# Graph attention: scores from turned rows in one product, four pairs a step, all steps written out

## What is computed

```python
def _L1_gnn_ref(x, edge_index, edge_attr, Wq, bq, Wk, bk, Wv, bv, We, Wskip, bskip, gamma, beta):
    ...
    q_all = x @ Wq.T + bq
    k_all = x @ Wk.T + bk
    v_all = x @ Wv.T + bv
    e = edge_attr @ We.T
    q = q_all[dst]
    k = k_all[src] + e
    v = v_all[src] + e
    scale = 1.0 / jnp.sqrt(jnp.asarray(d, dtype=x.dtype))
    alpha = (q * k).sum(-1) * scale
    amax = jax.ops.segment_max(alpha, dst, num_segments=N)
    ex = jnp.exp(alpha - amax[dst])
    denom = jax.ops.segment_sum(ex, dst, num_segments=N)
    w = ex / denom[dst]
    agg = jax.ops.segment_sum(v * w[:, None], dst, num_segments=N)
    out = agg + x @ Wskip.T + bskip
```

## Time and profile before

| | |
|---|---|
| median of 3 runs | 7149.32 us (7145.72 to 7151.49) |
| profiled execution | 7175.0 us, its span 7173.4 us |
| mean granted clock of TensorE | 0.811 of full |
| TensorE busy (PE) | 5774.2 us, 80% |
| VectorE busy | 4790.4 us, 67% |
| ScalarE busy | 3097.9 us, 43% |
| GpSimd busy | 1945.7 us, 27% |
| the chain that ended last | PE 40%, DVE 30%, issue 17%, another queue 6% |

### The profile page before, as it was taken

One profiled execution on the slowest core, in us unless ns is written; L12 is line 12 of the kernel. 1 busy time (PEld: TensorE's weight loads), 2 busy tenths in 40 slices (PEclk: granted clock), 3 DMA queues, 4 the chain that ended last, 5 costly groups with the idle time before them and its releaser, 6 DMA issues.

```text
span 7173.4 us, 145546 instructions
## 1 busy us (share of the span) xinstructions
PE 5774.2 (80%) x45481; PEld 4074.9 (57%) x45482; DVE 4790.4 (67%) x14785; ACT 3097.9 (43%) x8500; POOL 1945.7 (27%) x2110
## 2 busy tenths in 40 slices
PE   1499995577777777777777748999999999988998
PEld 0377773355555555555555526666666666654665
DVE  3888884565666666666666639999999999952001
ACT  0255554344444444444444434555555555520000
POOL 4011100455555555555555510000000000000110
PEclk6699997666666656656666668999999999978999
DMA  5255542222222222222222200000000000005664
GB/s 164 81 181 180 182 162 77 51 62 61 62 60 63 62 61 62 60 63 64 60 63 60 58 28 21 4 4 4 4 4 4 4 4 4 4 2 181 205 204 139
DMA packets 375578, 505.33 MB, mean 70 GB/s; under 512 B 258173, under 2 KB 303357, under 8 KB 355054
## 3 DMA queue, kind: packets, MB, share of 16 engines
q1 hardware_dynamic: 289631, 356.27, 15.3%
q0 software_dynamic: 82592, 141.23, 8.5%
q10 hardware_dynamic: 2738, 0.54, 0.0%
HBM read 341.26 MB, written 169.04 MB: 71 GB/s over the span
## 4 chain that ended last, share of the span: by engine, by line
PE 40%; DVE 30%; issue 17%; another core or an unknown queue 6%; ACT 2%; DVEq 2%; POOL 1%; DMA 1%; SPq 1%; ACTq 0%; POOLq 0%
PE psum L1213 36%; DVE R L708 8%; DVE HT L708 5%; DVE l L708 4%; DVE H L1101 3%; PE psum L1402 2%; DVE junk L1112 2%; DVE ACC L1086 2%; PE psum L1479 1%; DVEq L434 1%; DVE cols_pc L708 1%; DVE att L1075 1%; ACT H L1543 1%; DVE att L1112 1%
## 5 line engine op out<-in xcount | busy, mean ns | idle before, releaser
L1543 ACT ACTIVATE H<-psum 128x256 f32<-128x256 f32 (+2 forms) x1853 | 681.7, 391 | 1654.2 <-remote 565.7
L1213 PE MATMUL psum<-R 128*128 (+3 forms) x10946 | 1161.2, 260 | 85.5 <-DVE R L708 40.6
L1213 PE MATMUL psum<-R,HT 128*128 128x384 bf16 x6076 | 1084.3, 326 | 59.8 <-DVEq L1202 59.8
L1543 ACT ACTIVATE R<-psum 128x512 f32<-128x512 f32 (+4 forms) x1597 | 844.6, 543 | 537.9 <-PE psum L1213 488.1
L1213 PEld LDWEIGHTS psum<-R,G 128*128 128x128 bf16 x11840 | 735.0, 98 | 567.7 <-issue 334.9
L1213 PEld LDWEIGHTS psum<-R 128*128 128x128 bf16 x10946 | 834.9, 111 | 361.1 <-issue 158.0
L1213 PE MATMUL psum<-H 128*128 128x139 f32 (+1 forms) x3328 | 768.3, 352 | 322.2 <-DVE ACC L1086 153.3
L1213 PE MATMUL psum<-R,l 128*128 128x512 f32 (+1 forms) x1924 | 954.2, 578 | 67.0 <-DVE HT L708 64.5
L642 POOL DMA_INDIRECT H<-gather_table,idx_f x832 | 803.7, 966 | 590.4 <-remote 205.8
L642 POOL DMA_INDIRECT G<-gather_table,idx_f x832 | 787.2, 946 | 623.9 <-PE psum L1213 275.4
L1075 DVE TENSOR_TENSOR att<-att,col_f 128x1 f32<-128x1 f32 x1664 | 264.9, 159 | 960.5 <-remote 372.6
(11 more groups left out here) (227 smaller groups left out, 8124.9 us busy)
## 6 DMA issues: line engine op xcount, KB each, us to landing
adjacency_blocks<-HT SPq DMA_DIRECT2D x74, 1568.0 KB, 5.4
HT<-adjacency_blocks SPq DMA_DIRECT2D x50, 1568.0 KB, 6.6
H<-local_dst_pairs SPq DMA_DIRECT2D x104, 512.0 KB
R<-adjacency_blocks SPq DMA_DIRECT2D x24, 1568.0 KB, 6.5
G<-gather_table,idx_f POOLq DMA_INDIRECT x832
H<-gather_table,idx_f POOLq DMA_INDIRECT x832
node_sums<-G POOLq DMA_DIRECT2D x148, 64.0 KB
attr_pairs<-H SPq DMA_DIRECT2D x13, 640.0 KB, 7.0
```

The lines of the kernel that those rows point to most:

```text
L1213: return nc.tensor.matmul(o, lhs_t, rhs, start=start, stop=stop)
L1543: return nc.scalar.activation(o, a, f, **kw)
```

## The change

The attention stage is rewritten, in its arithmetic and in its order.

- **Scores by one product.** TensorE turns each gathered slot (`GT`, 128 rows, and the 11 extra columns as `GX`), ScalarE copies both, and the scores of a pair come straight as rows: queries of the window, turned (128 deep), times `GT`, plus the turned extras (11 deep) times `GX`, both float32, into one PSUM region. The one-hot matrices, `Q3`, VectorE's score product, the split into parts and its turning are gone. The queries' own product is now made turned, 13 blocks of up to four windows, into `QK` and `QX`.
- **Queries by transfer.** No engine reads a window's number but SyncE: it copies each pair's queries (128x128) and extras (11x128) from `QK` and `QX` into one of 16 places, six steps of four pairs ahead.
- **Sums by transfer.** VectorE adds into a ring of eight places (`sums`), each from the one before. SyncE writes every pair's place to `attention_sums` in DRAM, at the window's number for a window's last pair and at one of eight spare places otherwise (`put`). At the end the sums come back into `ACC` in four parts.
- **Corrections.** The differences of old and new maximum are made by VectorE for four pairs at once, and ScalarE takes one exponential for the four.
- **Four pairs a step, written out.** 416 steps and five more for the tail, no hardware loop. In step k TensorE makes the sum products of group k - 4, turns the exponentials of group k - 3, makes the scores of group k - 1 and turns the rows of group k. VectorE interleaves, pair by pair, the maximum of group k - 1 with the addition of group k - 4. The gathers need no copy of their indices.

The core of the diff (indentation cut by eight):

```diff
-Q3 = r1.bitcast(bf16)[:, 0:3 * W * FX].rearrange("p (t w f) -> p t w f", t=3, w=W)
+
 QT = accflat[:, 0:NP]
-member = r2b[:, 0:2 * CH * P].rearrange("p (u j e) -> p u j e", u=2, j=CH)
+QK = QT.rearrange("p (w n) -> p w n", n=P)
+QX = r1[0:X1, 0:NP].rearrange("p (w n) -> p w n", n=P)
+at = NP
+GT = r1[:, at:at + 2 * GR * P].rearrange("p (u j e) -> p u j e", u=2, j=GR)
+at += 2 * GR * P
+GX = r1[0:X1, at:at + 2 * GR * P].rearrange("p (u j e) -> p u j e", u=2, j=GR)
+at += 2 * GR * P
+masked = r1[:, at:at + 3 * GR * P].rearrange("p (j e) -> p j e", e=P)
...
+sums = hflat[:, at:at + AR * FX].rearrange("p (j f) -> p j f", f=FX)
+assert at + AR * FX <= NH
+queries = R2[:, 0:CH * P].rearrange("p (j n) -> p j n", n=P)
+at += AR * FX
+extras = [l2[0:X1, j * P:(j + 1) * P] for j in range(8)]
+extras += [accflat[0:X1, NP + j * P:NP + (j + 1) * P] for j in range(6)]
+extras += [hflat[0:X1, at + j * P:at + (j + 1) * P] for j in range(2)]
...
+    def load_rows(c):
+        if c >= 2:
+            sp.wait_ge(s_mem, c - 1)
+        rows = loc_p[c * CH:(c + 1) * CH, :].rearrange("(a j) e -> a (j e)", a=1)
+        sp.dma_start(locrow[:, c % 2, :], rows.broadcast_to([P, CH * P])).then_inc(s_lr[c % 2], 16)
+    def load_attrs(m):
+        if m >= 4:
+            sp.wait_ge(s_use, 8 * (m - 3))
+        h = m % 2 * CH // 2
+        sp.dma_start(G_att[m // 2 % 2][:, h:h + CH // 2, F + 1:FX],
+                     ea_p[m * CH // 2:(m + 1) * CH // 2, :].rearrange("j (e a) -> e j a", a=ED)).then_inc(s_ea[m % 4], 16)
+    def put_sums(k):
+        places = load_places(GR * k, GR)
+        for j in range(GR):
+            p = GR * k + j
+            sp.wait_ge(s_acc, p + 1)
+            sp.dma_start(sums_d.rearrange("(w n) f -> n w f", n=P)[:, bass.ds(places[j], 1), :].rearrange("n a f -> n (a f)"),
+                         sums[:, p % AR, :]).then_inc(s_fl[p % AR], 16)
+    def load_queries(k):
+        if k >= 4:
+            sp.wait_ge(s_row, k - 3)
+        numbers = load_windows(ENG.SP, GR * k, GR)
+        for j in range(GR):
+            a = (GR * k + j) % CH
+            sp.dma_start(queries[:, a, :], QK[:, bass.ds(numbers[j], 1), :].rearrange("p a n -> p (a n)")).then_inc(s_qw[k % 4], 16)
+            sp.dma_start(extras[a], QX[:, bass.ds(numbers[j], 1), :].rearrange("p a n -> p (a n)")).then_inc(s_qw[k % 4], 16)
+    for c in range(2):
+        load_rows(c)
+    for m in range(4):
+        load_attrs(m)
+    sp.wait_ge(s_qh, NB)
+    sp.wait_ge(s_qx, NB)
+    for k in range(6):
+        load_queries(k)
+    for k in range(GN):
+        put_sums(k)
+        if k + 6 < GN:
+            load_queries(k + 6)
+        if k % 4 == 3 and k // 4 + 2 < PC // CH:
+            load_rows(k // 4 + 2)
+        if k % 2 == 1 and k // 2 + 4 < PC * 2 // CH:
+            load_attrs(k // 2 + 4)
+    for k in range(AR):
+        sp.wait_ge(s_fl[k], 16 * (PC // AR))
+    for c in range(4):
+        w0_, w1_ = 4 * (NB * c // 4), min(W, 4 * (NB * (c + 1) // 4))
+        sp.dma_start(ACC[:, w0_:w1_, :], sums_d[w0_ * P:w1_ * P, :].rearrange("(w n) f -> n w f", n=P)).then_inc(s_back[c], 16)
...
-    for u in range(2):
-        gather(0, u, table, G_att)
-    loop(pool, gather, PC, table, G_att, first=2 * CH)
+    for p in range(PC):
+        if p % GR == 0 and p >= 2 * CH:
+            pool.wait_ge(s_use, p - 2 * CH + GR)
+        edge = bass.IndirectOffsetOnAxis(ap=idx_c[:, p:p + 1], axis=0)
+        pool.indirect_dma_start(out=slot(p)[:, 0:F], out_offset=None, in_=table, in_offset=edge).then_inc(s_g[p // GR % 8], 16)
...
+    for b, (w0_, n) in enumerate(BLK):
+        v.wait_ge(s_q, b + 1)
+        v.tensor_copy(QX[:, w0_:w0_ + n, :], psum[0:X1, 6 + b % 2, 0:n * P].rearrange("p (w n) -> p w n", n=P)).then_inc(s_qx, 1)
...
-    def attention_vector(i, k):
-        p = i + k
...
+    for k in range(GN + 5):
+        for j in range(GR):
+            p, q = GR * (k - 1) + j, GR * (k - 4) + j
+            if k - 1 in range(GN):
+                if p:
+                    v.wait_ge(s_min, p)
+                tt(oldm[:, p % CH:p % CH + 1], newm[:, (p - 1) % CH:(p - 1) % CH + 1], aux_c[:, p:p + 1],
+                   ALU.max).then_inc(s_nmo, 1)
+            if k - 4 in range(GN):
+                if j % 2 == 0:
+                    v.wait_ge(s_use, q + 2)
+                if j == 0:
+                    v.wait_ge(s_c, k - 3)
+                if q:
+                    v.wait_ge(s_acc, q)
+                if q >= AR:
+                    v.wait_ge(s_fl[q % AR], 16 * (q // AR))
+                v.scalar_tensor_tensor(sums[:, q % AR, :], sums[:, (q - 1) % AR, :], corr[:, q % CH:q % CH + 1],
+                                       psum[:, 6 + j // 2, j % 2 * FX:(j % 2 + 1) * FX], ALU.mult, ALU.add).then_inc(s_acc, 1)
+            if k - 1 in range(GN):
+                if j == 0:
+                    v.wait_ge(s_row, k)
+                    if k >= 4:
+                        v.wait_ge(s_et, k - 3)
+                    if p % CH == 0:
+                        v.wait_ge(s_mem, p // CH + 1)
+                v.wait_ge(s_nmo, p + 1)
+                v.tensor_tensor_reduce(out=masked[:, p % (3 * GR), :], in0=psum[:, 3 + (k - 1) % 2, j * P:(j + 1) * P],
+                                       in1=penalty[:, p // CH % 2, p % CH, :], scale=1.0, scalar=oldm[:, p % CH:p % CH + 1],
+                                       op0=ALU.add, op1=ALU.min, accum_out=newm[:, p % CH:p % CH + 1]).then_inc(s_min, 1)
+        if k - 1 in range(GN):
+            p = GR * (k - 1)
+            at = slice(p % CH, p % CH + GR)
+            v.wait_ge(s_min, p + GR)
+            tt(dif[:, at], newm[:, at], oldm[:, at], ALU.subtract).then_inc(s_dif, 1)
+            v.wait_ge(s_dif, 2 * k - 1)
+            v.scalar_tensor_tensor(dif[:, at], aux_c[:, p:p + GR], -1.0, dif[:, at], ALU.mult, ALU.min).then_inc(s_dif, 1)
+        if k % 4 == 3 and k // 4 + 1 < PC // CH:
+            mask_rows(k // 4 + 1)
...
-    def attention_tensor(i, k):
-        p = i + k
...
+    for b, (w0_, n) in enumerate(BLK):
+        if b >= 2:
+            t.wait_ge(s_qx, b - 1)
+            t.wait_ge(s_qh, b - 1)
+        mm(psum[:, 4 + b % 2, 0:n * P], C[:, 0:F], QT[:, w0_ * P:(w0_ + n) * P])
...
+    for k in range(GN + 5):
+        if k - 4 in range(GN):
+            t.wait_ge(s_etc, k - 3)
+            if k >= 5:
+                t.wait_ge(s_acc, GR * (k - 4))
+            for j in range(GR):
+                mm(psum[:, 6 + j // 2, j % 2 * FX:(j % 2 + 1) * FX], ET[:, j, :], slot(GR * (k - 4) + j)).then_inc(s_use, 1)
+        if k - 3 in range(GN):
+            t.wait_ge(s_exp, GR * (k - 2))
+            if k >= 4:
+                t.wait_ge(s_etc, k - 3)
+            for j in range(GR):
+                last_ins = nc.tensor.transpose(bank4(5)[:, j, :], masked[:, (GR * (k - 3) + j) % (3 * GR), :], ident[:, :])
+            last_ins.then_inc(s_et, 1)
+        if k - 1 in range(GN):
+            t.wait_ge(s_gt, k)
+            if k >= 3:
+                t.wait_ge(s_min, GR * (k - 2))
+            t.wait_ge(s_qw[(k - 1) % 4], 128 * ((k - 1) // 4 + 1))
+            for j in range(GR):
+                o, a = bank4(3 + (k - 1) % 2)[:, j, :], (GR * (k - 1) + j) % CH
+                mm(o, queries[:, a, :], GT[:, (k - 1) % 2, j, :], stop=False)
+                last_ins = mm(o, extras[a], GX[:, (k - 1) % 2, j, :], start=False)
+            last_ins.then_inc(s_row, 1)
+        if k in range(GN):
+            t.wait_ge(s_g[k % 8], 64 * (k // 8 + 1))
+            if k % 2 == 0:
+                t.wait_ge(s_ea[k // 2 % 4], 16 * (k // 8 + 1))
+            if k >= 1:
+                t.wait_ge(s_gt, k)
+            for j in range(GR):
+                nc.tensor.transpose(bank4(k % 2)[:, j, :], slot(GR * k + j)[:, 0:F], ident[:, :])
+            for j in range(GR):
+                last_ins = nc.tensor.transpose(bank4(2)[0:X1, j, :], slot(GR * k + j)[:, F:FX], ident[:, :])
+            last_ins.then_inc(s_t, 1)
...
+    for k in range(GN + 4):
+        if k - 3 in range(GN):
+            act.wait_ge(s_et, k - 2)
+            if k >= 4:
+                act.wait_ge(s_use, GR * (k - 3))
+            activation(ET, bank4(5), ACT.Copy).then_inc(s_etc, 1)
+        if k - 2 in range(GN):
+            for j in range(GR):
+                p = GR * (k - 2) + j
+                act.wait_ge(s_min, p + 1)
+                e = masked[:, p % (3 * GR), :]
+                activation(e, e, ACT.Exp, bias=newm[:, p % CH:p % CH + 1], scale=-1.0).then_inc(s_exp, 1)
+            act.wait_ge(s_dif, 2 * k - 2)
+            at = slice(GR * (k - 2) % CH, GR * (k - 2) % CH + GR)
+            activation(corr[:, at], dif[:, at], ACT.Exp).then_inc(s_c, 1)
+        if k in range(GN):
+            act.wait_ge(s_t, k + 1)
+            if k >= 2:
+                act.wait_ge(s_row, k - 1)
+            activation(GX[:, k % 2], bank4(2)[0:X1], ACT.Copy)
+            activation(GT[:, k % 2], bank4(k % 2), ACT.Copy).then_inc(s_gt, 1)
```

More of the change, by code:

```diff
@@ L25 @@
 GR = 4
+AR = 8
 TABLES = 8
```

(41 more changed lines are left out.)

260 lines of the change are left out of this document (38 added, 222 removed).

## The result

The changed kernel takes **9441.8 us** (median of 4 runs, 9437 to 9449) against 7148.6 before: 1.321 times as long, 95% interval 1.319 to 1.323. The forecast was 8590 with a range to 9150. The direction was right. The time is 852 us over the forecast and 292 us over the end of the range.

The account below looks back on a forecast made before the run. The attention step was taken as a loop of TensorE's and VectorE's parts, 11.9 us at the low clock and 8.0 at the full, mixed 10.2, with SyncE's 8.5 hidden. 4349 + 416 x 10.2 gave 8590 us, range 7780 to 9150.

Parts of the forecast that it names:

- SyncE's sum: SyncE's transfer issues and register loads in an attention step: 8.5 us, bounds 6.2 and 9.8, hidden below a 10.2 us step.
- the forecast's own formula: Whole kernel: median = 4349 + 416 s, with s the attention step in us; s = 10.2 gives 8590 us.
- The differences of maxima and the mask come after that and lie beside TensorE: VectorE's work after the fourth addition of a step, claimed to overlap TensorE and left out of VectorE's 2.97 us.
- If SyncE never waits: Sign that the forecast is wrong: SyncE was expected to have spare time at attention_added in the attention steps.
- TensorE waiting for the queries' transfers: Sign that the forecast is wrong: TensorE waits for queries_of_pairs_loaded; queries, issued six groups ahead, were expected in time.
- The paid turns of depth: Eight score products a step, alternating 128 and 11 rows: 0.73 us each low, 0.41 full; 5.8 and 3.3 us together.
- The rival with free turns: Depth changes among score products cost nothing; loop 9.5 us low, 6.4 full, SyncE sets the step: 7885 us, chance 0.12.
- VectorE's part: From the scores through four minimum and addition pairs until TensorE resumes: 2.97 us a step, 0.86 a pair.
- TensorE's part: From a step's first sum product to its last score: 8.95 us at the low clock, 5.0 at the full one.
- The clock: TensorE's clock in the attention, full for 33% of the time, mixing steps of 11.9 and 8.0 us into 10.2.
- The constant: Everything outside the 416 attention steps, with changes at start, pipe and end: 4349 us of the median.
- a low clock throughout: Rival: TensorE's clock stays low in the attention, step 11.9 us, 9300 us in all; chance 0.08.

Follow-up runs that it names:

- e1: Changed kernel with SyncE's load of the local row numbers issued three of its steps earlier: 9009.3 us, 1.367 times the kernel before.
- e6: As e5, with the extras' products taking all 128 rows, zero-padded, so no depth changes among the scores: 8405.1 us, 1.275 times the kernel before.
- e8: As e6, with the extras not loaded after the first six steps (part of the data wrong): 7321.9 us, 1.110 times the kernel before.
- e0: The changed kernel unchanged, run on another chip as the measure for the other runs: 9385.3 us, 1.423 times the kernel before.
- e5: Changed kernel with both edits of e1 and e3, row numbers earlier and extras moved as 128 partitions: 8366.8 us, 1.269 times the kernel before.
- e10: As e1, with queries and extras not loaded after the first six steps (part of the data wrong): 8227.8 us, 1.248 times the kernel before.
- e9: As e6, everything computed, with the extras' loads issued by ScalarE in place of SyncE: 7424.1 us, 1.126 times the kernel before.
- e7: As e6, with queries and extras not loaded after the first six steps (part of the data wrong): 6799.1 us, 1.031 times the kernel before.
- e3: Changed kernel with the extras' transfers moving 128 partitions in place of 11, products still 11 deep: 8910.9 us, 1.352 times the kernel before.
- e12: As e9, with SyncE loading the numbers of windows and places for two steps at once: 7373.4 us, 1.118 times the kernel before.
- e11: As e7, with the extras' products 32 rows deep in place of 128: 7999.1 us, 1.212 times the kernel before.

## Why the prediction was wrong, and where it was right

**SyncE's sum was mis-sized; this is the step that failed.** The forecast had 8.5 us a step, 9.8 as its upper end, and called it hidden below 10.2. Measured: 11.3 (e1), more than any bound given. The terms: twelve transfers at 0.50 are 6.0, and measured about 8.6, since the extras' 11-row issue takes 0.82 us plus 0.1 to 0.2 around it, and the queries' 0.53 plus 0.1; the rows taken for it were attributes, adjacency blocks and a weight matrix, and no transfer of 11 rows stood in the trace. The register loads at 0.95 came out as 0.87 and 1.09, as assumed. With 11.3 in place of 8.5 the forecast's own formula gives 4349 + 416 x 11.3 = 9050. From e6 to e8 the step follows that queue one to one.

**"The differences of maxima and the mask come after that and lie beside TensorE"** was wrong at the mask. The mask waits for a transfer that SyncE issues only after it has put out the sums of that same VectorE step and then loaded the queries of another; the prediction never put the two program orders side by side. Price by e1: 376 us (1.0 us a step, SyncE's wait). The rest of the stop is time in which SyncE makes up for its lateness. 9050 + 376 = 9426, against 9442 measured.

**"If SyncE never waits"** was named in the prediction as a sign that it is wrong, and it is nearly what the trace shows: 426 us of waiting in 5110. Another such sign, TensorE waiting for the queries' transfers, does not show in the changed kernel (e0) and appears only where the stop is gone (e1, 355 us).

**The paid turns of depth were right.** Forecast 0.73 low and 0.41 full, measured 0.72 and 0.42 in the attention itself, 11 rows like the 1 row. The rival with free turns had the wrong depth but the right size: with 128 rows it is 0.22. Where SyncE sets the step they cost nothing, though (e5 and e6). The changed kernel itself was not run with the padding alone; its mean step too is SyncE's, so there the largest term of the forecast's sum was most likely a true price that the mean does not show.

**VectorE's part** was 2.97 and is 2.50 (4020.74 to 4023.24 by the timeline), a pair 0.76 and not 0.86. **TensorE's part** was 8.95 low and is 8.5 (e10) to 8.9 (the changed kernel, to VectorE's start); the loop is 11.06 low and 7.3 full (e10) instead of 11.9 and 8.0.

**The clock** of the loop, full for a third of the time: e10 shows 0.65, which is full for 30%. The loop alone takes 9.42 us, so the forecast's 10.2 was 8% too long in itself; it lies below SyncE's 11.3 either way. In the changed kernel the clock is 0.60. The direction did not hang on SyncE: the loop alone makes the kernel 1.25 times as long as before (e10), as the forecast's terms for TensorE and VectorE had it.

**The constant** 4349 is right to 20 us: 9442 - 416 x 12.29 = 4329. DMA bandwidth was no limit: share 0.31, and 0.69 in e9.

**The range** ended at 9150, and the one case beyond it was a low clock throughout (9300). What happened, SyncE over its upper price, was in no case: 0.60 a transfer was taken from issues of other shapes and could not bound a kind that the trace did not have.

## What to carry to other kernels

Price the issuing queue transfer by transfer: a queue that only starts copies can be the bound at 12 starts a step, and a start of 11 partitions cost 0.82 us where 128 partitions cost 0.53. When loads are issued from a program that also waits for results, write the two programs' orders side by side at the steps where they meet: a load that stands behind a put of the same step as its reader stops everyone. Where engines take turns in being late, look at single steps too: here three ran at one engine's pace and the fourth paid for another's. Let consecutive products keep one depth, padded with zeros; but take away what sets the step first, or the gain is not seen (e6 gave nothing, e7 gave 1429 us).

## What the runs showed of the hardware

- A transfer of 11 partitions takes SyncE 0.82 us to issue (e1), one of 128 partitions from the same places 0.535 us (e3), though it moves twelve times the bytes.
- A register load on SyncE costs 0.21 us a number and 0.1 for the load itself: four 0.93 (e9), eight 1.76 (e12).
- Padding a product's depth from 11 to 32 rows doesn't remove the idle before its weight load, 0.22 us at the low clock (e10, e11); padding it to the depth of its neighbours, 128, does (e7).
- TensorE's clock didn't go by its busy share. With the changes of depth (e10) TensorE was busy 5.70 of 7.20 us in a stretch at the full level (79%), and the clock still fell to 1.2 GHz and was there most of the time (0.65); without them (e7) it was busy 71% and nearly always at 2.4 GHz (0.98). What the clock answers to, these runs don't show.
- One chip gave the kernel before a mean clock of 0.81, four others 0.87 to 0.88: 7149 us against 6591 to 6597, 8% apart. The changed kernel, with 0.60 and 0.61 in its attention, took 9442 and 9385.
